# One fold per part, sums beside PSUM, selectors in place and corner weights by ScalarE in a four-stage convolution kernel

## The reference

```python
x = x + _L0_conv_ref(_gn(x), ...)   # 3x3 convolution in Winograd form, 6x6 frequencies
x = x + _L1_conv_ref(_gn(x), ...)   # deformable 3x3 convolution
x = x + _L2_conv_ref(_gn(x), ...)   # quantised residual block, four 3x3 convolutions
x = x + _L3_conv_ref(_gn(x), ...)   # convolution + vertical edges, channel attention
```

```python
py = hs + ky + dy ; px = ws + kx + dx
sampled = _bilinear_sample(x, py, px)        # four corners, weighted, zero outside
y = einsum('bgikhw,goik->bgohw', s, wg) + b  # 8 groups
```

## Time and profile before

| what | value |
|---|---|
| median of 3 runs | 4327.13 us |
| all runs | 4340.27, 4327.13, 4326.23 us |
| span of the profiled execution | 4328.9 us |
| PE, DVE, ACT, POOL busy | 4115.4, 3191.3, 1827.2, 3159.8 us |
| share of the span | 95%, 74%, 42%, 73% |
| DMA | 1022.57 MB, mean 236 GB/s |
| PE's granted clock | 0.983 of full speed in the mean |

### The profile page before, as it was taken

One profiled execution on the slowest core, in us unless ns is written; L12 is line 12 of the kernel. 1 busy time (PEld: TensorE's weight loads), 2 busy tenths in 40 slices (PEclk: granted clock), 3 DMA queues, 4 the chain that ended last, 5 costly groups with the idle time before them and its releaser, 6 DMA issues.

```text
span 4328.9 us, 61705 instructions
## 1 busy us (share of the span) xinstructions
PE 4115.4 (95%) x21925; PEld 1924.0 (44%) x21925; DVE 3191.3 (74%) x6460; ACT 1827.2 (42%) x2008; POOL 3159.8 (73%) x3094
## 2 busy tenths in 40 slices
PE   2899999999999999999999999999999999999993
PEld 2444444444444444444444444444444444444441
DVE  4757787777877777787777877877787777877663
ACT  1344444444444434444444444444444444444431
POOL 1777777777777777777777777777777777777750
PEclk8899999999999999999999999999999999999996
DMA  4677787878878788887877878787887878878762
GB/s 111 216 234 245 238 263 220 265 227 248 256 235 263 227 250 258 245 256 229 261 233 246 270 233 261 223 251 249 245 258 232 258 234 253 260 237 258 240 194 64
DMA packets 480231, 1022.57 MB, mean 236 GB/s; under 512 B 262164, under 2 KB 298356, under 8 KB 475636
## 3 DMA queue, kind: packets, MB, share of 16 engines
q1 hardware_dynamic: 283252, 460.40, 34.7%
q10 hardware_dynamic: 98400, 356.97, 25.4%
q0 software_dynamic: 98304, 201.52, 16.5%
HBM read 862.19 MB, written 73.20 MB: 216 GB/s over the span
## 4 chain that ended last, share of the span: by engine, by line
PE 72%; DVE 13%; POOL 5%; issue 4%; DMA 3%; SPq 1%; ACTq 1%; ACT 1%; POOLq 0%; DVEq 0%
PE ps_r L1506 52%; PE ps_c L1492 5%; POOL ring L599 5%; PE ps_y L1521 4%; PE ps_a L1445 3%; DVE col_hat L1198 2%; PE ps_c L1535 2%; PE ps_a L1492 2%; DMA taps_c<-plane_act 1%; PE ps_y L1542 1%; DVE ps_w L1219 1%; DVE ring L1225 1%; PE ps_a L1483 1%; DVE ring L1221 1%; ACTq L793 1%
## 5 line engine op out<-in xcount | busy, mean ns | idle before, releaser
L599 POOL DMA_INDIRECT ring<-patch_table,idx_part x3072 | 3151.6, 1026 | 1031.6 <-issue 1019.6
L1506 PE MATMUL ps_r<-select,image 128*128 128x512 f32 x6912 | 3160.9, 602 | 21.1 <-DVE col_hat L1198 15.3
L1506 PEld LDWEIGHTS ps_r<-select,image 128*128 128x128 f32 x6912 | 1253.6, 190 | 1424.3 <-issue 1368.9
L1198 DVE TENSOR_TENSOR col_hat<-ps_r,col_hat 128x512 f32<-128x512 f32 x1152 | 790.6, 686 | 919.1 <-PE ps_r L1506 917.8
L649 ACT ACTIVATE select<-row_in,minus_row 128x1536 f32<-128x1536 f32 x384 | 604.8, 1575 | 1042.7 <-PE ps_r L1506 556.9
L651 ACT ACTIVATE select<-select,one_col 128x1536 f32<-128x1536 f32 x384 | 605.3, 1576 | 12.5
L668 ACT COPY samples<-ps_c 128x512 f32<-128x512 f32 x256 | 148.9, 582 | 655.8 <-PE ps_c L1535 655.8
L1219 DVE TENSOR_TENSOR ps_w<-ring,ps_w 128x384 f32<-128x384 f32 x512 | 284.8, 556 | 19.8 <-DMA ring<-patch_table,idx_part 15.2
L1225 DVE TENSOR_TENSOR ring<-ring,ps_w 128x384 f32<-128x384 f32 x512 | 280.3, 547 | 4.4
L1221 DVE TENSOR_TENSOR ring<-ring,ps_w 128x384 f32<-128x384 f32 x512 | 280.2, 547 | 0.0
L1521 PEld LDWEIGHTS ps_y<-col_hat,w_dense 128*32 128x32 f32 x6144 | 143.5, 109 | 297.5 <-issue 245.9
(11 more groups left out here) (233 smaller groups left out, 2588.9 us busy)
## 6 DMA issues: line engine op xcount, KB each, us to landing
col_hat<-coord_table SPq DMA_DIRECT2D x384, 768.0 KB
row_in<-coord_table ACTq DMA_DIRECT2D x384, 768.0 KB
ring<-patch_table,idx_part POOLq DMA_INDIRECT x3072
taps_c<-plane_act SPq DMA_DIRECT2D x135, 268.1 KB
coord_table<-wino ACTq DMA_DIRECT2D x64, 216.0 KB
taps_c<-xn_c ACTq DMA_DIRECT2D x96, 130.0 KB
taps_c<-xn_c SPq DMA_DIRECT2D x96, 130.0 KB
plane_act<-act_c SPq DMA_DIRECT2D x180, 65.0 KB
```

The costliest lines, as they stand in the source:

```text
L599: nc.gpsimd.indirect_dma_start(out=ring[j][:, h % 2, k, :], out_offset=None, in_=table, in_offset=bass.IndirectOffsetOnAxis(ap=idx_part[:, ...
L1198: v.tensor_tensor(hat_t, ps_r[:, (s + t) % 2], hat_t, ALU.mult).then_inc(tile_weighed, 1)
L1506: ins = mm(ps_r[:, (s + t) % 2], image[:, m, t], select[s % 2][:, m], start=(m == 0), stop=(m == PAIRS - 1))
```

## The change

- `SUMMED` and `sum_tiles` go. In every slot DVE keeps the first tile's product in `col_hat`; the second and the third product are written back to `ps_r` and then added to the running sum, `dense_sum[:, e]`, a new buffer for the 3 slots of a part. The tile counts as weighed, and frees its half of `ps_r`, after the add.
- PE folds a part's three sums once, in the first slot of the next part and after its second row tile, together with the folds of the gathered taps: 12 small matmuls a part.
- The row coordinates are loaded straight into `select`, of which there are now 3, and both ACT operations work in place. `row_in` goes. A load waits until PE has used the selector that lay there. In ACT's slot the load for slot s+2 now comes behind the making of selector s+1.
- The part's corner weights are copied to PSUM by ACT instead of DVE, at the head of its slot, and DVE waits for that.
- In stage L2 ACT's scaled results of the second to fourth convolution stay in PSUM (`ps_c`), and DVE's first rounding step works there, in two halves; PE's turns of slots 11, 14 and 17 wait for that reading. The absolute value of the edges goes from DVE to ACT (128x1024). Some DVE steps change their third: the sum `add_conv`, moments, spread of image n-1's L2 norm, and the edge difference.

The core of the diff:

```diff
@@ SP, load_cols
-                    sp.wait_ge(dense_folded, n * SLOTS + s - 2)
+                    sp.wait_ge(tile_weighed, (n * SLOTS + s - 2) * WT)
@@ ACT
-                if not known_zero(n) or s >= 2:
-                    act.wait_ge(row_in_read, n * SLOTS + s - 1)
+                if not known_zero(n) or s >= 3:
+                    act.wait_ge(rows_made, (n * SLOTS + s - 2) * WT)
...
-                nc.scalar.dma_start(row_in[s % 2][:].rearrange("p m x -> p (m x)"),
+                nc.scalar.dma_start(select[s % 3][:].rearrange("p m x -> p (m x)"),
...
             def make_select(n, s):
-                u = n * SLOTS + s
-                act.wait_ge(row_in_in[s % 2], (n * (SLOTS // 2) + s // 2 + 1) * 16)
-                if not known_zero(n) or s >= 2:
-                    act.wait_ge(rows_made, (u - 1) * WT)
-                sel = select[s % 2][:]
-                nc.scalar.activation(sel, row_in[s % 2][:], ACT.Abs, bias=minus_row[:]).then_inc(row_in_read, 1)
-                act.wait_ge(row_in_read, u + 1)
+                act.wait_ge(rows_in[s % 3], (n * (SLOTS // 3) + s // 3 + 1) * 16)
+                sel = select[s % 3][:]
+                nc.scalar.activation(sel, sel, ACT.Abs, bias=minus_row[:]).then_inc(distance_made, 1)
+                act.wait_ge(distance_made, n * SLOTS + s + 1)
                 nc.scalar.activation(sel, sel, ACT.Relu, bias=one_col[:], scale=-1.0).then_inc(select_made, 1)
...
+            def take_weights(n, g):
+                if g == 0:
+                    act.wait_ge(a_dve.sem, a_dve.at(n, "weights"))
+                if not known_zero(n) or g > 0:
+                    act.wait_ge(weighted, (n * PARTS + g) * JB + RING)
+                nc.scalar.copy(w_part, w_cur[:].rearrange("p (j g) k m -> p g j k m", g=PARTS)[:, g]).then_inc(weights_taken, 1)
...
+                if s == 21:
+                    act.wait_ge(c_dve.sem, c_dve.at(n, "edges"))
+                    nc.scalar.activation(t_d, t_d, ACT.Abs).then_inc(c_act.sem, 1)
...
-                if s != SLOTS - 2:
-                    rows_ahead(n, s)
+                after = (n, g + 1) if g < PARTS - 1 else (n + 1, 0)
+                if e == DT - 1 and live(after[0]):
+                    take_weights(*after)
...
                     make_select(n + (s + 1) // SLOTS, (s + 1) % SLOTS)
+                if s != SLOTS - 2:
+                    rows_ahead(n, s)
@@ DVE, weigh_tile
-                hat_t = col_hat[s % 3][:, t]
-                v.tensor_tensor(hat_t, ps_r[:, (s + t) % 2], hat_t, ALU.mult).then_inc(tile_weighed, 1)
+                hat_t, rows_t = col_hat[s % 3][:, t], ps_r[:, (s + t) % 2]
+                if t == 0:
+                    v.tensor_tensor(hat_t, rows_t, hat_t, ALU.mult).then_inc(tile_weighed, 1)
+                    return
+                g, e = divmod(s, DT)
+                chain.step(v.tensor_tensor(rows_t, rows_t, hat_t, ALU.mult))
+                dve.wait_ge(tile_weighed, tile)
+                if t == 1 and e == 0 and (not known_zero(n) or g > 0):
+                    dve.wait_ge(dense_folded, n * PARTS + g)
+                first_term = col_hat[s % 3][:, 0] if t == 1 else dense_sum[:, e]
+                v.tensor_tensor(dense_sum[:, e], first_term, rows_t, ALU.add).then_inc(tile_weighed, 1)
...
+            def rounded_plus_psum(dst, rest):
+                for h in range(2):
+                    chain.add(v.tensor_scalar(ps_c[:, h], ps_c[:, h], M, M + 127.0, ALU.add, ALU.min))
+                chain.join()
+                for h in range(2):
+                    half = slice(h * HALF, (h + 1) * HALF)
+                    ins = stt(dst[:, half], ps_c[:, h], M - 127.0, rest[:, half], ALU.max, ALU.subtract)
+                    if h == 0:
+                        chain.add(ins)
+                return ins
...
-                if at == (0, 2):
+                if at == (1, 0):
                     add_conv(n)
-                if at == (1, 0):
+                if at == (1, 1):
                     moments(x2, bn_c, mv_c, c_dve.sem)
-                if at == (2, 0):
+                if at == (2, 1):
                     spread(mv_c, ps_c[:, 0, 0:1], n, "2", c_dve, c_pe)
@@ PE
+                for e in range(DT):
+                    pe.wait_ge(tile_weighed, (n * SLOTS + g * DT + e + 1) * WT)
                     for j in range(JB):
                         ins = mm(ps_y[j * C:(j + 1) * C, :],
                                  w_dense[:, DT - 1 - e].rearrange("p g o -> p (g o)"),
-                                 col_hat[s % 3][:, t, j * P:(j + 1) * P], start=(e == 0 and t == 0), stop=False)
+                                 dense_sum[:, e, j * P:(j + 1) * P], start=(e == 0), stop=False)
...
-                    if q == 0:
-                        fold_before(n, s)
+                    if q == 1 and e == 0:
+                        fold_before(n, g)
```

More of the change, by code:

```diff
@@ L41 @@
 DSEL = DT * Q
-SUMMED = (4, 5, 6, 7, 8, 11, 14, 19, 20, 21, 22, 23)
 ITEMS = DT * PARTS
@@ L231, in build @@
         w_cur = sb("w_cur", [P, Q, GTAPS, CORNERS])
-        row_in = [sb(f"row_in{b}", [P, PAIRS, HALF]) for b in range(2)]
-        select = [sb(f"select{b}", [P, PAIRS, HALF]) for b in range(2)]
+        select = [sb(f"select{b}", [P, PAIRS, HALF]) for b in range(3)]
         col_hat = [sb(f"col_hat{b}", [P, WT, HALF]) for b in range(3)]
+        dense_sum = sb("dense_sum", [P, DT, HALF])
         image = sb("image", [P, PAIRS, WT, P])
@@ L295, in build @@
         coords_out = sem("coords_out")
-        row_in_in = [sem(f"row_in_in{b}") for b in range(2)]
+        rows_in = [sem(f"rows_in{b}") for b in range(3)]
         col_hat_in = [sem(f"col_hat_in{b}") for b in range(3)]
@@ L1225, in add_rows @@
                 return chain.add(v.tensor_tensor(upper, upper, lower, ALU.add))
-            def take_weights(g):
-                return chain.add(v.tensor_copy(w_part, w_cur[:].rearrange("p (j g) k m -> p g j k m", g=PARTS)[:, g]))
             def add_columns(n, g, j):
@@ L1363, in c @@
                     normalise(inner_c, x3, mv_c, n, "3", c_dve, c_act)
-                if at == (21, 1):
+                if at == (20, 2):
                     dve.wait_ge(halo_c, n * 32 + 32)
                     dve.wait_ge(c_dve.sem, c_dve.at(n, "norm3"))
-                    chain.add(v.tensor_tensor(rows(td_), rows_c[:, 0:RS, 0:W], rows_c[:, 2:RS + 2, 0:W],
-                                              ALU.subtract))
-                if at == (21, 2):
-                    chain.join()
-                    stt(td_, td_, -1.0, td_, ALU.mult, ALU.max).then_inc(c_dve.sem, 1)
+                    v.tensor_tensor(rows(td_), rows_c[:, 0:RS, 0:W], rows_c[:, 2:RS + 2, 0:W],
+                                    ALU.subtract).then_inc(c_dve.sem, 1)
                 if at == (23, 1):
@@ L1505, in row_tile, with fold_dense @@
                 for m in range(PAIRS):
-                    ins = mm(ps_r[:, (s + t) % 2], image[:, m, t], select[s % 2][:, m], start=(m == 0),
+                    ins = mm(ps_r[:, (s + t) % 2], image[:, m, t], select[s % 3][:, m], start=(m == 0),
                              stop=(m == PAIRS - 1))
                 ins.then_inc(rows_made, 1)
-            def fold_dense(n, s):
-                g, e = divmod(s, DT)
-                if e == 0 and (not known_zero(n) or g > 0):
+            def fold_dense(n, g):
+                if not known_zero(n) or g > 0:
                     pe.wait_ge(conv_saved, n * PARTS + g)
-                for t in range(1 if s in SUMMED else WT):
-                    if s in SUMMED:
-                        pe.wait_ge(tiles_summed, n * len(SUMMED) + SUMMED.index(s) + 1)
-                    else:
-                        pe.wait_ge(tile_weighed, (n * SLOTS + s) * WT + t + 1)
+                for e in range(DT):
+                    pe.wait_ge(tile_weighed, (n * SLOTS + g * DT + e + 1) * WT)
                     for j in range(JB):
@@ L1617, in slot, with fold_before @@
                         first(n + 2, s, q)
-            def fold_before(n, s):
-                n, s = (n, s - 1) if s > 0 else (n - 1, SLOTS - 1)
+            def fold_before(n, g):
+                n, g = (n, g - 1) if g > 0 else (n - 1, PARTS - 1)
                 if not live(n):
                     return
-                fold_dense(n, s)
-                g, e = divmod(s, DT)
-                if e == DT - 1:
-                    for k in range(CHUNKS):
-                        fold(n, g, k)
+                fold_dense(n, g)
+                for k in range(CHUNKS):
+                    fold(n, g, k)
             schedule(pe, Chain(pe, None), slot, prepare_rest)
```

50 lines of the change are left out of this document (22 added, 28 removed).

## The result

The changed kernel takes 4468.6 us (median of 4 runs, 4463.06 to 4478.82) against 4332.97 for the kernel before on the same chip (4326.23 to 4340.27): a ratio of 1.0315, 95% interval 1.0295 to 1.0335. It is slower by 136 us. Forecast were 4410, a range of 4290 to 4480, and 0.72 for slower. The direction came true, and so did VectorE's lag as its main cause; the size was too small by 59 us, for two reasons that the sum did not hold: what stands behind the weights copy on ScalarE, and TensorE's clock.

A forecast was written before the change was run, and what follows sets the result against it. TensorE sets the pace, VectorE and POOL close behind. Per image, 246.6 us of work plus 15.3 of stalls is +4.8, with 0.7 for ScalarE 5.5; times 15 is 83 on 4328.9, less 1.8: 4410 us, range 4290 to 4480.

The forecast's parts named there:

- VectorE's lag: VectorE's added sums make it late at TensorE in crowded slots: 4370 to 4450 us, chance 0.60.
- the sum: Tile-by-tile reckoning of TensorE's work plus stalls: 261.9 us an image; with ScalarE's 0.7 and the median, 4410 us in all.
- PE's saving: Fewer folds on TensorE: 13.9 us an image become 6.4, saving 7.5; its work falls to 246.6.
- VectorE's prices: VectorE's 24 product-and-sum pairs cost 0.73 us each extra, 17.4 an image; its work rises from 199.9 to 216.4.
- the rival of dearer PSUM operands: VectorE's PSUM operands cost 0.1 us more at each of 48 operations: 4458 us; 0.12 together with the row-load rival.
- The rounding in halves: VectorE's rounding as two 512-element scalings from PSUM: bounds no change and 0.6 us more; taken, 0.7 x 3 = 2.0 an image.
- The stalls, 15.3 us an image: TensorE's waits for VectorE after the change, mostly in slots 1 to 4, 8 to 10 and 15 to 18; 3.2 before.
- the rule: Over 72 tiles, a row tile starts when TensorE is free and the tile two before is released; each stall costs 0.16 more.
- ACT's share: Row loads behind ScalarE's selectors, its copies and edge operation cost 0.7 us an image, bounds 0 and 5.
- The bound of 5 us: Upper bound an image on ScalarE's 0.7 us cost, where row loads come late behind plane copies and in slots 22 and 23.
- The rival of 5 us an image: Row loads come late in slots 3 to 5 and 22 to 23: 4475 us; 0.12 together with the PSUM-operand rival.
- The faster rival: VectorE's extra work is hidden, unstretched gathers need 250 us an image and TensorE 249.8: 4220 us, chance 0.21.

The follow-up runs named there:

- e1: The changed kernel without the sums VectorE gained in the 12 slots not summed before (first and third products lost there): 4371.6 us.
- e5: The kernel before with all 24 slots summed in SBUF instead of 12, nothing else of the change: 4403.7 us, ratio 1.0170.
- e4: The changed kernel with products written to SBUF, so a tile's half of `ps_r` is released after the product, before the sum: 4461.1 us.
- e3: The changed kernel with ScalarE making the attention vector before it waits for the next weights in slot 23: 4401.8 us.
- e7: The kernel before with the selectors made in place in 3 buffers and each row load behind the selector before it, nothing else: 4447.8 us.
- g1: The changed kernel without the added sums in 12 slots and with the attention vector made ahead of the weights: 4332.9 us, ratio 0.9994.
- g3: The kernel before with 15 chosen slots summed and, in these, the second and third product left in PSUM: 4297.8 us, ratio 0.9923.
- e6: The kernel before with 15 slots summed instead of 12, chosen by VectorE's room: 4323.2 us, ratio 0.9977.
- f3: The kernel before with selectors made in place and the row load at the head of ScalarE's slot: 4402.4 us, ratio 1.0169.
- g4: The kernel before with selectors in place and their load behind them, slot 12's row load cut from 768 KB to 32 KB: 4446.3 us.

## Why the prediction came out as it did

- **PE's saving, 7.5 us an image: right.** PE is busy 248.1 us in the image at full clock, 246.6 plus the extra length of its stalled tiles. The folds' records fell to 3072.
- **VectorE's prices: right.** The pair of product and sum is 0.72 us from start to start (2205.18 - 2204.46 below), with PSUM on both sides, so the rival of dearer PSUM operands fell. The rounding in halves, which no row of before showed, is two scalings, 1.29 together, and two halves of the second step, again 1.29: 0.60 + 0.07 more than in the earlier trace rows, where I had put 0.7. So scaling 512 elements in PSUM takes as long as 1024 in SBUF, the upper of the two bounds. VectorE's total was to be about 3440 us and is 3422.8. Its timeline after:

```profile
2098.06 1.29 DVE L1293 TENSOR_SCALAR ps_c<-ps_c 128x512 f32<-128x512 f32 x2
2099.38 1.29 DVE L1297 SCALAR_TENSOR_TENSOR work_c<-ps_c,work_c 128x512 f32<-128x512 f32 x2
...
2204.46 0.69 DVE L1213 TENSOR_TENSOR ps_r<-ps_r,col_hat 128x512 f32<-128x512 f32 x1
2205.18 0.69 DVE L1218 TENSOR_TENSOR dense_sum<-col_hat,ps_r 128x512 f32<-128x512 f32 x1
```

- **The stalls, 15.3 us an image: right to within 2 us, and in place.** PE is idle 16.0, but 2.4 of it is the attention vector, which the sum did not have; that the totals are so near each other is luck. The other 13.6 lie where the rule had them (image from 2253 to 2522 us, the forecast in brackets): 2.3 in slots 1 to 4 (3.6), 5.5 in 8 to 10 (6.0), 1.0 in 12 to 14 (1.3), 3.4 in 15 to 18 (3.2), 1.3 in 19 to 21 (1.2). e1 and e5 tie them to the sums, and e4 rules out the moment of release.
- **The term that failed: ACT's share, "0.7 us an image".** I costed its eight weight copies only in slot 21, and didn't name what is queued behind the copy in slot 23: the attention vector, a table load of 1.28 us, and PE's turn. That is 2.4 us of stall. The bound of 5 us would have covered it, but I had tied that bound to the row loads alone. That 4468.6 lies inside the range is luck as well: its upper end of 4480 was set for row loads that cost 5 us an image, and in the changed kernel they did not.
- **The term that was missing: the clock.** No stall in the earlier trace rows is over 1.1 us and the clock in the earlier trace rows is 1.00; I priced a stall at its own length plus 0.16. Stalls of 1.65 us and more often cost 1.7 us more, 5.1 in the image above and 4.2 in the mean. With the attention stall away and one drop left (e3) the kernel takes 4402 and an image 263.0, where the sum had 4410 and 261.9.
- **The row loads.** The rival of 5 us an image did not come true in the changed kernel, where they cost little: the waits of ACT's selectors for a load rose from 45 to 105, but PE waited only 6.5 us for `samples` and 1.1 for the taps. Alone they cost 121 us (e7), and in g1 about the whole saving. Two causes of lateness in one image are not added up: where VectorE makes TensorE late, the taps and the samples are there, or nearly, by the time they are asked for.
- **The faster rival** needed VectorE's work to be hidden: refuted by e5. Its other half was right: the gathers are relieved (1.000 us against 1.026; forecast nearer 0.99), of which e4 gives 0.016 to the sums in PSUM, and g3 turns that into 25 of its 35 us; the other 10 are e6's choice of slots.

## What to carry to other kernels

An engine with a quarter of its time free can still be full in the slots that matter: carry the two engines' work forward tile by tile before moving work between them, and add it only where the lead is (15 chosen slots 0.2% faster, with their products in PSUM 0.8%, all 24 slots 1.7% slower). When a wait moves to another engine, list everything queued behind it on that engine up to the next thing the bound engine needs. A transfer that is moved probably delays another engine's transfer without any wait of its own (argued here, not shown); look at what is issued within a microsecond of it.

## What the hardware showed that I had not expected

- TensorE's granted clock fell to its lower level (0.50, 1.2 GHz), mostly for 3.4 us, in e7 and others also for 6.8, at stalls of 1.6 to 5.4 us in which it did nothing, and came back to 1.00. Not at each: of two stalls of 1.79 us in (10, 2), one image apart, one was followed by full speed, and one of 1.81 us ahead of row tile (10, 1) at 2366 too. Between 640 and 3990 us the changed kernel has 60 stalls of over 1.6 us and 30 drops, e3 50 and 9, f3, whose stalls are mostly longer than 2.7 us, 14 and 13. What decides stays open. Removing one stall an image (e3) gave 67 us for the 33.7 us that it lasted.
- Two transfers of 768 KB and 804 KB on different queues shared the DMA engines (g4: 55.2% and 40.6% in the same 3.2 us). Where TensorE waited for them, the taps took 12.2 to 15.6 us with a row load issued up to 1.6 us ahead of them and 10.4 to 11.9 with none within 7.7 us.
